# A graph-attention kernel's tile loop: groups of 12 tiles instead of 8, a ring of two groups, one-hots turned by a five-row product

## The chip, the cores and the metric

One core of one Trainium2 chip. The metric is device time in microseconds (us), the median of three runs. The engines go by their names in the profile: PE is TensorE (matrix products; PEld its weight loads), DVE is VectorE, ACT is ScalarE, POOL is GpSimd, SP is SyncE. A name with a q (ACTq) is that engine's instruction queue.

## The reference

A graph-attention layer with four heads over 12,500 nodes and 200,000 edges, added to its input and layer-normalised:

```
feats  = relu(x @ W1 + b1) @ W2 + b2
hid    = relu(concat(feats[row], feats[col], weight) @ A1 + ab1)
e      = leaky_relu(hid @ A2 + ab2, 0.2);   w = exp(e - max(e))
pooled = segment_sum(w * feats[col], row) / (segment_sum(w, row) + 1e-10)
out    = layernorm(x + concat_heads(pooled))
```

## The kernel before, in words

Ahead of the loop the kernel computes two tables over the nodes, one for the row side (`p_table`) and one for the column side (`qf_table`, 776 numbers a node: 516 of the hidden layer, 260 of the features), and sorts the edges by windows of 125 row nodes. A tile is 128 edges of one window, one edge on each partition. There are 1,664 tiles.

The tile loop takes groups of 8 tiles (`SB`), with a ring of 24 tile slots, so of three groups. A step `k` of the loop has one piece on each engine, and the pieces work on different groups, because each engine's instructions stand in one fixed order and meet others only by semaphores. In step `k`:

- POOL gathers the table rows of group `k+1` tile by tile from `qf_table` (L761); each waits until the sum of the tile that held its slot is done.
- ACT makes the one-hots of group `k+1`: edge by window node, four tiles at a time (`onehots`: four Abs L1220, a small copy L1222, one Relu L1224). PE turns them by four transposes (`turn`, L1016), and ACT takes the turned ones out of PSUM (`take_turned`, L1209). The three last rows of a turned one-hot (125 to 127) hold the edge weight in three parts and come with the transposes.
- PE forms the hidden layer of group `k` tile by tile (`hidden_src`: six products of the turned one-hot with the window's table L1003, two with the gathered rows L1007). At the first tile of each four it waits for `take_turned`. DVE adds the gathered half to it (L1596) and takes four dot products (L1606).
- For group `k-1` DVE finds the new running maximum, the shift: three small operations beside tile 0, two beside tile 1 (L1632, L1636), two beside tile 2 (`new_shift` L1642, `shifted` L1646). PE helps twice, after its tiles 2 and 3 (`max_t` L1022, `max_to_all` L1027). Then ACT takes exponentials (`exps`, L1198) and weights the features tile by tile, four activations a tile (`weight`, L1191).
- PE sums the weighted features of group `k-2` by the one-hot (`sum_up`, L990), tile `j` beside its hidden tile `j`, and DVE adds the sums into the window's accumulator (L1655).

ACT's order within a step is: `take_turned(0,1)`, `onehots(1,0)`, `exps`, the load of the records two groups ahead (L1229), then the eight `weight`s, with `take_turned(1,0)` behind the first and `onehots(1,1)` behind the fifth. In a call such as `take_turned(0,1)` the first number is the group relative to `k`, the second the batch of four tiles in it. SP loads the next window's table (L596) as windows are finished. After the loop the shifts of all groups correct the accumulators, and the layer norm follows.

Of the kernel before, what the change touches and what calls it, by code (L numbers as in the profile page):

```python
# [25 lines left out]
I32 = mybir.dt.int32  # L26
# [4 lines left out]
def gnn_layer(nc, x, src, dst, weight, W1, b1, W2, b2, A1, ab1, A2, ab2, out):  # L31
# [30 lines left out]
    SB = 8  # L62
    RING = 24
    SPB = RING // SB
    NT = (E + W * (P - 1)) // P
    NT = -(-NT // SB) * SB
    NSB = NT // SB
    BODIES = NSB // SPB - 1
# [3 lines left out]
    HALF_SB = SB // 2  # L72
# [14 lines left out]
    CHUNKS = NT * P // S  # L87
    sorted_rows = nc.dram_tensor("sorted_rows", (CHUNKS + 3 * P, SF), F32, kind="Internal").ap()
    records = nc.dram_tensor("records", (P * NT, 4), F32, kind="Internal").ap()
    base_rows_d = nc.dram_tensor("base_rows", (BLOCKS, 2, CB * W), BF16, kind="Internal").ap()  # L90
    shift_rows = nc.dram_tensor("shift_rows", (NSB, H), F32, kind="Internal").ap()

    ctx = ExitStack()
    with ctx:
# [14 lines left out]
        iota_row = sb("iota_row", [P, WN])  # L109
# [4 lines left out]
        onehot = sb("onehot", [P, RING, P])  # L114
        onehot_t = sb("onehot_t", [P, SB, P], BF16)
        rec = sb("rec", [P, RING, 4])
# [10 lines left out]
        shift_all = sb("shift_all", [P, NSB, H])  # L127
        last_sb = sb("last_sb", [P, W], I32)
        end_prev = sb("end_prev", [1, W], I32)
        win_pack = sb("win_pack", [1, NT // 4], I32)  # L130
# [3 lines left out]
        win_of = onehot[0:1, :, :].rearrange("p t n -> p (t n)").bitcast(I32)[:, 0:NT]  # L134
        row_tmp = onehot_t[0:1, :, :].rearrange("p t n -> p (t n)").bitcast(I32)[:, 0:NT // 4]
        assert NT <= RING * P
# [105 lines left out]
        rec_all = z[:, 0:NT * 4].rearrange("p (t n) -> p t n", n=4)  # L242
# [5 lines left out]
        shift_flat = shift_all[:, :, :].rearrange("p s h -> p (s h)")  # L248
# [18 lines left out]
        s_row_field = sem("s_row_field")  # L267
# [20 lines left out]
        s_win_iota = sem("s_win_iota")  # L288
        s_stage = [sem(f"s_stage{n}") for n in range(4)]
        s_field_mm = sem("s_field_mm")  # L290
        s_dst_low = sem("s_dst_low")
        s_field_a = sem("s_field_a")
        s_field_b = sem("s_field_b")
        s_rec_st = sem("s_rec_st")
# [5 lines left out]
        s_passed_c = sem("s_passed_c")  # L300
# [10 lines left out]
        s_bias_part = sem("s_bias_part")  # L311
# [13 lines left out]
        s_rec = [sem(f"s_rec{n}") for n in range(SPB)]  # L325
        s_row_dist = sem("s_row_dist")
        s_onehot = sem("s_onehot")
# [28 lines left out]
        s_c_const = sem("s_c_const")  # L356
# [17 lines left out]
        SC = next(NSB // n for n in range(1, NSB) if NSB % n == 0 and NSB // n <= P)  # L374
        KS = NSB // SC
# [38 lines left out]
        N_TAB_STEPS = 13  # L414
# [5 lines left out]
        BULK = NT // P  # L420
        assert BULK * P == NT
# [64 lines left out]
        def _(sp):  # L486
# [86 lines left out]
            for g in range(BULK):  # L573
                sp.wait_ge(s_field_a, g + 1)
                sp.wait_ge(s_field_b, g + 1)
                sp.dma_start(rec_d[:, g * P * 4:(g + 1) * P * 4], rec_all[:, g * P:(g + 1) * P, :].rearrange("p t n -> p (t n)")).then_inc(s_rec_st, 16)
                if g + 4 < BULK:
                    sp.wait_ge(s_field_mm, g + 1)
                    load_stage(g + 4)
            sp.wait_ge(s_a_rows, 16 * 6)  # L580
            sp.wait_ge(s_tab_step, N_TAB_STEPS)
            sp.wait_ge(s_rec_st, 16 * BULK)
            sp.dma_start(rec[:, 0:SB, :].rearrange("p t n -> p (t n)"), rec_d[:, 0:SB * 4]).then_inc(s_rec[0], 16)
            sp.wait_ge(s_rec[0], 16)
# [18 lines left out]
            sp.wait_ge(s_shift_all, NSB)  # L603
            sp.dma_start(shift_rows.rearrange("(a s) h -> a (s h)", a=1), shift_flat[0:1, :]).then_inc(s_c_shifts, 16)
# [16 lines left out]
        def _(pool):  # L621
# [7 lines left out]
            pool.iota(iota_row[:, :], [[1, WN]], base=1, channel_multiplier=0, allow_small_or_imprecise_dtypes=True).then_inc(s_const, 1)  # L629
# [13 lines left out]
            pool.tensor_scalar(minus_b, ident[:, :], -1.0, None, ALU.mult).then_inc(s_bias_part, 1)  # L643
# [3 lines left out]
            pool.wait_ge(s_masks, 1)  # L647
# [4 lines left out]
            pool.tensor_scalar(fields[0:EP, :, 0], edge_t[0:EP, :], 1.0, None, ALU.add).then_inc(s_row_field, 1)  # L652

            pool.wait_ge(s_weights, N_W)
            pool.wait_ge(s_row_field, 1)
# [11 lines left out]
            pool.wait_ge(s_masks, 2)  # L667
# [27 lines left out]
            pool.tensor_copy(hml[rows3, 0, :], bias).then_inc(s_bias_part, 1)  # L695
            pool.wait_ge(s_bias_part, 2)
            pool.tensor_tensor(rest[rows3, 0, :], bias, hml[rows3, 0, :], ALU.subtract).then_inc(s_bias_part, 1)
            pool.wait_ge(s_bias_part, 3)
            pool.tensor_copy(hml[rows3, 1, :], rest[rows3, 0, :]).then_inc(s_bias_part, 1)
            pool.wait_ge(s_bias_part, 4)  # L700
            pool.tensor_tensor(hml[rows3, 2, :], rest[rows3, 0, :], hml[rows3, 1, :], ALU.subtract).then_inc(s_bias_part, 1)
            pool.wait_ge(s_bias_part, 5)
            pool.tensor_scalar(rest[rows3, 0, :], hml[rows3, 0, :], ident[rows3, 0:1], None, ALU.mult).then_inc(s_bias_part, 1)
            pool.wait_ge(s_bias_part, 6)
            pool.tensor_scalar(rest[rows3, 1, :], hml[rows3, 1, :], ident[rows3, 1:2], None, ALU.mult).then_inc(s_bias_part, 1)
            pool.wait_ge(s_bias_part, 7)
            pool.tensor_tensor(rest[rows3, 0, :], rest[rows3, 0, :], rest[rows3, 1, :], ALU.add).then_inc(s_bias_part, 1)
            pool.wait_ge(s_bias_part, 8)
            pool.tensor_scalar(rest[rows3, 1, :], hml[rows3, 2, :], ident[rows3, 2:3], None, ALU.mult).then_inc(s_bias_part, 1)
            pool.wait_ge(s_bias_part, 9)  # L710
# [1059 lines left out]
```

## Time and profile before

| | |
|---|---|
| median of 3 runs | 4588.38 us (4586.27 to 4588.84) |
| the profiled execution | 4587.18 us, span of its instructions 4585.4 us |
| mean granted TensorE clock | 0.977 of full speed |
| the tile loop | from about 1312 us to 4468 us of the span |

The span is the time from the first to the last instruction; the execution's own time is 1.8 us longer. An engine's busy time says how much work it has; which engine sets the time of a stretch is read from who waits for whom there.

### The profile page before, as it was taken

To read this page: it belongs to the slowest core of one execution; us is meant where nothing else is said; L and a number is where in the kernel's file an instruction comes from. 1 tells how busy PE (TensorE), PEld (TensorE's weight loads), DVE (VectorE), ACT (ScalarE), POOL (GpSimd) and SP (SyncE) were. 2 spreads that over 40 slices of the span, in tenths; PEclk is the share of its full clock that TensorE was granted. 3 is DMA by queue.
4 is the path that set the end of the run, shared out by engine and by line. 5 is a ranking of instruction groups with operands and counts; after the bars stand their busy time and mean duration, and the time that the engine had idled before them with its cause. 6 is when DMAs were issued, how large, how long until landed. Compare 5 with 4: busy or idle time off the path is not lost.

```text
span 4585.4 us, 128801 instructions
## 1 busy us (share of the span) xinstructions
PE 4132.6 (90%) x25516; PEld 2946.2 (64%) x25517; DVE 4094.2 (89%) x21278; ACT 3319.3 (72%) x11283; POOL 2340.7 (51%) x2495
## 2 busy tenths in 40 slices
PE   2599999999889999999999999999999999999990
PEld 1255555555567777777777777777777777777760
DVE  8888888888779999999999999999999999999988
ACT  1244444444468888888888888888888888888875
POOL 5444444444445555555555555555555555555535
PEclk9799999999989999999999999999999999999995
DMA  2144444444477777777777777777777777777757
GB/s 90 42 99 89 104 96 91 102 96 93 99 220 224 228 223 226 222 224 226 225 224 223 225 227 221 225 225 226 226 220 223 227 226 223 223 226 224 218 157 224
DMA packets 266911, 851.78 MB, mean 186 GB/s; under 512 B 107916, under 2 KB 109584, under 8 KB 266861
## 3 DMA queue, kind: packets, MB, share of 16 engines
q0 software_dynamic: 169920, 673.54, 52.8%
q1 hardware_dynamic: 63543, 160.18, 11.7%
q10 hardware_dynamic: 33398, 17.49, 1.5%
q8 instruction: 20, 0.33, 0.0%
q14 instruction: 30, 0.25, 0.0%
HBM read 739.10 MB, written 111.90 MB: 186 GB/s over the span
## 4 chain that ended last, share of the span: by engine, by line
PE 38%; ACT 28%; issue 3%; DVE 2%; DMA 0%; ACTq 0%; POOL 0%; DVEq 0%; SPq 0%; POOLq 0%
ACT z L1191 19%; PE psum L1003 16%; PE psum L1007 9%; PE psum L990 9%; ACT onehot L1220 4%; ACT onehot_t L1209 3%; PE psum L1016 3%; ACT onehot L1224 2%; PE psum L971 1%; DVE z L1727 1%; DVE z L1720 1%; PE psum L1027 0%; ACT onehot L1222 0%; DVE z L1743 0%; DVE z L1738 0%
## 5 line engine op out<-in xcount | busy, mean ns | idle before, releaser
L761 POOL DMA_INDIRECT z<-qf_table,rec x1664 | 1605.9, 965 | 1458.8 <-PE psum L990 1038.6
L1191 ACT ACTIVATE z<-z 128x64 f32<-128x64 f32 x6656 | 1651.1, 335 | 0.0
L1003 PE MATMUL psum<-p_win,onehot_t 128*128 x9984 | 1409.7, 274 | 87.2 <-ACT onehot_t L1209 67.0
L1003 PEld LDWEIGHTS psum<-p_win,onehot_t 128*128 128x128 bf16 x9984 | 966.5, 97 | 541.6 <-issue 213.0
L990 PE MATMUL psum<-z,onehot 128*128 128x260 f32 x3328 | 1031.9, 392 | 3.8 <-DVE acc L1655 3.5
L1007 PE MATMUL psum<-z,ident 128*128 128x258 f32 x3328 | 1002.2, 383 | 0.0
L1606 DVE SCALAR_TENSOR_TENSOR z<-z,a_b 128x129 f32<-128x129 f32 x3328 | 881.4, 289 | 3.7 <-issue 0.2
L1606 DVE SCALAR_TENSOR_TENSOR z<-psum,a_b 128x129 f32<-128x129 f32 x3328 | 827.5, 286 | 0.0
L721 POOL DMA_INDIRECT sorted_rows<-z x300 | 475.0, 1583 | 635.9 <-DVE z L1484 487.3
L1596 DVE TENSOR_TENSOR z<-z,psum 128x258 f32<-128x258 f32 x1664 | 698.0, 419 | 98.5 <-PE psum L1007 97.2
L1655 DVE TENSOR_TENSOR acc<-acc,psum 125x260 f32 x1664 | 701.5, 422 | 26.2 <-PE psum L990 4.1
L990 PEld LDWEIGHTS psum<-z,onehot 128*128 128x128 f32 x3328 | 577.2, 190 | 97.5 <-DVE acc L1655 24.7
L1209 ACT ACTIVATE onehot_t<-psum 128x512 bf16<-128x512 f32 x416 | 243.6, 586 | 444.3 <-PE psum L1016 444.3
L1220 ACT ACTIVATE onehot<-iota_row,rec 128x125 f32<-128x125 f32 x1664 | 525.6, 389 | 19.3 <-PE psum L990 13.4
L1007 PEld LDWEIGHTS psum<-z,ident 128*128 128x128 f32 x3328 | 501.9, 190 | 20.4
L1426 DVE TENSOR_REDUCE z<-psum 125x4 f32<-125x400 f32 x400 | 229.0, 572 | 186.8 <-PE psum L833 182.9
L868 PE MATMUL psum<-acc 128*128 128x500 f32 x800 | 377.4, 593 | 0.0
L1111 ACT ACTIVATE acc<-psum,acc 128x500 f32<-128x500 f32 x200 | 135.6, 678 | 279.5 <-PE psum L868 279.5
L1471 DVE TENSOR_TENSOR acc<-z 125x1280 bf16<-125x1280 bf16 x400 | 327.0, 818 | 1.9 <-issue 1.9
L1133 ACT ACTIVATE acc<-psum 125x516 bf16<-125x516 f32 x300 | 181.6, 605 | 184.1 <-PE psum L896 104.7
L1016 PE MATMUL psum<-ident,onehot 128*128 128x128 f32 x1664 | 261.5, 280 | 55.9 <-ACT onehot L1224 55.9
L1224 ACT ACTIVATE onehot<-onehot,ones_f 128x500 f32<-128x500 f32 x416 | 298.1, 717 | 0.0
(230 smaller groups left out, 4602.9 us busy)
## 6 DMA issues: line engine op xcount, KB each, us to landing
p_table<-acc SPq DMA_DIRECT2D x100, 338.6 KB
p_win<-p_table SPq DMA_DIRECT2D x100, 338.6 KB
z<-qf_table,rec POOLq DMA_INDIRECT x1664, 4.5
qf_table<-acc SPq DMA_DIRECT2D x75, 339.5 KB
acc<-in_x_dram SPq DMA_DIRECT2D x25, 448.0 KB
z<-in_x_dram SPq DMA_DIRECT2D x20, 560.0 KB
out_dram<-z ACTq DMA_DIRECT2D x20, 560.0 KB
qf_table<-z SPq DMA_DIRECT2D x25, 339.5 KB
```

What stands on the lines that cost most here:

```text
L721: pool.indirect_dma_start(out=sorted_rows, out_offset=bass.IndirectOffsetOnAxis(ap=row_i[0:KB[k], (b - 3) % 2, k:k + 1], axis=0), in_=rows ...
L761: pool.indirect_dma_start(out=z_t[:, o + j, :], out_offset=None, in_=qf_table, in_offset=bass.IndirectOffsetOnAxis(ap=rec[:, o + j, 3:4].b ...
L990: pe.matmul(psum[:, 4 + j % 2, 0:H * HF], onehot[:, slot, :], z_t[:, slot, ZW:QW], start=True, stop=True)\
L1003: mm = pe.matmul(to, onehot_t[:, j, :], p_flat[:, bass.ds((w % 2) * (3 * ZW) + (part * ZW + o), n)], start=(part == 0), stop=(part == 2 an ...
L1007: mm = pe.matmul(z_two(slot), ident[:, :], z_t[:, slot, NA:ZW], start=False, stop=True, skip_group_check=True)
L1016: mm = pe.transpose(psum[:, 6, j * P:(j + 1) * P], onehot[:, ((k + off) * SB + u * HALF_SB + j) % RING, :], ident[:, :])
L1191: op = act.activation(z_t[:, slot, o:o + DO], z_t[:, slot, o:o + DO], ACT.Copy, scale=z_t[:, slot, o + DO:o + HF])
L1220: op = act.activation(onehot[:, oo + j, 0:WN], iota_row[:, :], ACT.Abs, scale=-1.0, bias=rec[:, oo + j, 0:1])
L1224: act.activation(onehot[:, oo:oo + HALF_SB, 0:WN], onehot[:, oo:oo + HALF_SB, 0:WN], ACT.Relu, scale=-1.0, bias=ones_f[:, 0:1]).then_inc(s ...
L1596: dve.tensor_tensor(own, own, z_one(slot), ALU.add).then_inc(s_z_added, 1)
L1606: return dve.scalar_tensor_tensor(out=own, in0=of, scalar=0.0, in1=a2_b[:, h * AT:(h + 1) * AT], op0=ALU.max, op1=ALU.mult, accum_out=e_ra ...
L1655: dve.tensor_tensor(a, a, psum[0:WN, 4 + j % 2, 0:H * HF], ALU.add).then_inc(s_acc, 1)
```

## The change

Groups have 12 tiles (three batches of four), and the ring of 24 slots holds two groups. The tiles become 1,668 and the groups 139. The transposes go: PE makes the turned one-hot by one product of five rows, since 1 - (e - n)^2 = 2ne - e^2 + 1 - n^2 is 1 where edge row e is node n and at most 0 elsewhere. The five rows of the edges (e, and e^2 in two parts, with two rows of ones) are loaded for a whole group by `load_edges`; ACT's `take_turned` becomes a Relu out of PSUM. The three rows of edge weights no longer come with it: each `take_turned` sends a DMA of three rows by four tiles into rows 125 to 127 (`s_edge_w`), and PE waits for it at the first tile of the batch. The one-hot that is not turned is made a group later, just before it is used (`onehots` works on group `k-1`, the small copy is gone), from rows that `load_rows` loads. The chain to the new shift is spread over DVE's tiles 0, 2 and 3 and PE's tiles 3 and 4. PE's and DVE's sums run seven tiles behind the group's start: tile `j` of group `k-1` beside tile `j+7` of step `k`, the last seven in the next step. Records shrink from four numbers to two, and are loaded one group ahead. The stage that writes records ahead of the loop writes the new rows too.

```diff
-    SB = 8
+    SB = 12
+    BATCH = 4
+    NBATCH = SB // BATCH
+    LAG = 7
     RING = 24
...
                 def gather(j):
...
-                    if live(i, k, -2):
-                        pool.wait_ge(s_agg, tile(-2, j) + 1)
+                    if live(i, k, -1):
+                        pool.wait_ge(s_agg, tile(-1, j) + 1)
...
                 def hidden_src(j):
...
-                    if j % HALF_SB == 0:
-                        pe.wait_ge(s_oht, (i * SPB + k) * 2 + (j // HALF_SB + 1))
+                    if j % BATCH == 0:
+                        pe.wait_ge(s_oht, (i * SPB + k) * NBATCH + (j // BATCH + 1))
+                        pe.wait_ge(s_edge_w[j // BATCH], (i * SPB + k) * 16 + 16)
...
                 def turn(off, u):
-                    for j in range(HALF_SB):
-                        mm = pe.transpose(psum[:, 6, j * P:(j + 1) * P], onehot[:, ((k + off) * SB + u * HALF_SB + j) % RING, :], ident[:, :])
-                    mm.then_inc(s_oht_mm, 1)
+                    if u == 0:
+                        pe.wait_ge(s_edge_k[kn], i * 16 + ((k + off) // SPB + 1) * 16)
+                    since(pe, s_oht, batch)
+                    pe.matmul(psum[0:WN, 6, 0:BATCH * P], node_k[:, 0:WN], edge_k[:, kn, u * BATCH:(u + 1) * BATCH, :].rearrange("p t n -> p (t n)"),
+                              start=True, stop=True).then_inc(s_oht_mm, 1)
...
-                if live(i, k, -3):
-                    sum_up(-3, SB - 1)
                 for j in range(SB):
                     if live(i, k, 0):
                         hidden_src(j)
-                    if j == SB // 4 and live(i, k, 0):
+                    if j == 2 and live(i, k, 0):
                         turn(0, 1)
-                    if j == SB // 4 and live(i, k, -1):
+                    if j == 3 and live(i, k, -1):
                         max_t()
-                    if j == SB // 4 + 1 and live(i, k, -1):
+                    if j == 4 and live(i, k, -1):
                         max_to_all()
-                    if j == SB - SB // 4 and live(i, k, 1):
+                    if j == 6 and live(i, k, 0):
+                        turn(0, 2)
+                    if j == 10 and live(i, k, 1):
                         turn(1, 0)
...
-                    if j < SB - 1 and live(i, k, -2):
-                        sum_up(-2, j)
+                    if j < LAG and live(i, k, -2):
+                        sum_up(-2, j + SB - LAG)
+                    if j >= LAG and live(i, k, -1):
+                        sum_up(-1, j - LAG)
...
                 def take_turned(off, u):
...
+                    act.dma_start(onehot_t[WN:P, own, :],
+                                  row_feats[bass.ds(tile(off, u * BATCH), BATCH), 3:6, :].rearrange("t f n -> f t n")).then_inc(s_edge_w[u], 16)
+                    act.wait_ge(s_oht_mm, batch + 1)
+                    act.activation(onehot_t[0:WN, own, :].rearrange("p t n -> p (t n)"), psum[0:WN, 6, 0:BATCH * P], ACT.Relu).then_inc(s_oht, 1)
...
+                def load_edges():
+                    act.dma_start(edge_k[0:3, kn, :, :], row_feats[bass.ds((i * SPB + (k + 1)) * SB, SB), 0:3, :].rearrange("t f n -> f t n"))\
+                       .then_inc(s_edge_k[kn], 16)
...
+                if live(i, k, -1):
+                    onehots(0)
+                if live(i, k, 1):
+                    load_edges()
                 if live(i, k, 0):
                     take_turned(0, 1)
-                if live(i, k, 1):
-                    onehots(1, 0)
                 if live(i, k, -1):
                     exps()
-                if live(i, k, 2):
+                if live(i, k, 1):
                     load_records()
                 for j in range(SB):
                     if live(i, k, -1):
                         weight(j)
-                    if j == 0 and live(i, k, 1):
+                    if j in (3, 7) and live(i, k, -1):
+                        onehots(j // BATCH + 1)
+                    if j == 3 and live(i, k, 0):
+                        take_turned(0, 2)
+                    if j == 7 and live(i, k, 1):
+                        load_rows()
                         take_turned(1, 0)
-                    if j == SB // 2 and live(i, k, 1):
-                        onehots(1, 1)
...
-                chain = {0: [(-1, bias), (-1, leaky), (-1, tiles_max)], 1: [(-1, heads_max), (-1, diagonal)],
-                         2: [(-1, new_shift), (-1, shifted)]}
+                chain = {0: [(-1, bias), (-1, leaky), (-1, tiles_max)], 2: [(-1, heads_max), (-1, diagonal)],
+                         3: [(-1, new_shift), (-1, shifted)]}
```

## Rows read from the trace of the kernel before

**Rows 1.** The page's first part: busy us, share, instructions of each engine.
```profile
PE 4132.6 (90%) x25516; PEld 2946.2 (64%) x25517; DVE 4094.2 (89%) x21278; ACT 3319.3 (72%) x11283; POOL 2340.7 (51%) x2495
```

**Rows 2.** 2000:3000: busy PE, PEld, DVE, ACT, POOL, clock, DMA share, GB/s; L1655's group.
```profile
2000.00:3000.00 1000.00, 957.52 (x6034) 725.54 (x6033) 934.26 (x5899) 854.86 (x3176) 544.40 (x663) 1.00 0.77 224
...
L1655 DVE TENSOR_TENSOR acc<-acc,psum 125x260 f32 x531 | 223.9, 422 | 6.8
```

**Rows 3.** Timeline, ScalarE, one group of 8: start, us, engine, line, what [idle before].
```profile
2501.68 0.60 ACT L1209 ACTIVATE onehot_t<-psum 128x512 bf16<-128x512 f32 x1 [1.91 <-PE psum L1016]
...
2502.17 3.92 ACT L1191 ACTIVATE z<-z 128x64 f32<-128x64 f32 x16
...
2505.99 1.26 ACT L1220 ACTIVATE onehot<-iota_row,rec 128x125 f32<-128x125 f32 x4
...
2510.77 0.57 ACT L1209 ACTIVATE onehot_t<-psum 128x512 bf16<-128x512 f32 x1
...
2511.34 1.27 ACT L1220 ACTIVATE onehot<-iota_row,rec 128x125 f32<-128x125 f32 x4
...
2512.64 0.72 ACT L1224 ACTIVATE onehot<-onehot,ones_f 128x500 f32<-128x500 f32 x1
...
2512.78 0.34 ACTq L1229 DMA_DIRECT2D rec<-records  x1
...
2513.26 0.24 ACT L1198 ACTIVATE z<-e_sh 128x32 f32<-128x32 f32 x1
...
2513.54 1.06 ACT L1191 ACTIVATE z<-z 128x64 f32<-128x64 f32 x4
...
2516.78 0.60 ACT L1209 ACTIVATE onehot_t<-psum 128x512 bf16<-128x512 f32 x1 [2.18 <-PE psum L1016]
```

**Rows 4.** Timeline, TensorE and VectorE, the same group.
```profile
2509.10 0.82 PE L1003 MATMUL psum<-p_win,onehot_t 128*128 x6
...
2511.09 0.19 DVE L1646 TENSOR_TENSOR e_sh<-e_val,shift 128x32 f32<-128x32 f32 x1
...
2511.78 0.94 PE L1003 MATMUL psum<-p_win,onehot_t 128*128 x6 [0.48 <-ACT onehot_t L1209]
...
2512.99 0.60 PE L990 MATMUL psum<-z,onehot 128*128 128x260 f32 x2
...
2513.43 0.82 PE L1003 MATMUL psum<-p_win,onehot_t 128*128 x6
...
2514.97 0.82 PE L1003 MATMUL psum<-p_win,onehot_t 128*128 x6
```

**Rows 5.** DMA view, ScalarE's queue: packets from 2512.78 to 2514.28, 2515.28, 2515.78.
```profile
q10 hardware_dynamic: 1, 0.00, 0.1%
...
q10 hardware_dynamic: 78, 0.01, 2.5%
...
q10 hardware_dynamic: 144, 0.02, 3.8%
```

**Rows 6.** The chain of waits, two transfers outside the tile loop: start, us.
```profile
1310.41 1.78 DMA rec<-records
...
4468.45 1.16 DMA shift_rows<-shift_all
```

**Rows 7.** DMA view, 704.08 to 705.33, ScalarE's queue, one two-row load.
```profile
q10 hardware_dynamic: 4, 0.01, 2.3%
```

**Rows 8.** Line 761, the gathers, 2000 to 3000 us.
```profile
DMA to landing us min/median/max: 3.8/4.5/7.1
```

**Rows 9.** TensorE by timeline, by chain, by windows (busy, granted clock, DMA share, GB/s).
```profile
1303.65 2.84 PE L971 MATMUL psum<-ident,z 128*128 128x128 f32 x12
...
1316.42 1.47 PE psum L1003 x6
...
1307.50:1310.00 2.50, 0.00 (x0) 0.78 0.28 105
...
1317.50:1320.00 2.50, 2.50 (x12) 0.67 0.94 340
```

More of the change, by code:

```diff
@@ L373, in gnn_layer @@
         CR = 5
-        SC = next(NSB // n for n in range(1, NSB) if NSB % n == 0 and NSB // n <= P)
-        KS = NSB // SC
+        SC = next(NSH // n for n in range(1, NSH) if NSH % n == 0 and NSH // n <= P)
+        KS = NSH // SC
         assert CGROUPS * CG == W and CGROUPS % CR == 0
@@ L413, in gnn_layer @@
         N_PARTS = 5
-        N_TAB_STEPS = 13
+        N_TAB_STEPS = 14
+        assert SB == 12 and all(t * 683 >> 13 == t // SB for t in range(NT))
         EMPTY_W = CHUNKS // P * SF
@@ L702, in _ @@
[L702 to L707, printed above, removed]
@@ L1203, in take_turned @@
                 def take_turned(off, u):
-                    group = (i * SPB + (k + off)) * 2 + u
-                    act.wait_ge(s_oht_mm, group + 1)
+                    batch, own = (i * SPB + (k + off)) * NBATCH + u, slice(u * BATCH, (u + 1) * BATCH)
                     if live(i, k, off - 1):
-                        act.wait_ge(s_z_mm, tile(off - 1, u * HALF_SB + HALF_SB - 1) + 2)
-                    act.activation(onehot_t[:, u * HALF_SB:(u + 1) * HALF_SB, :].rearrange("p t n -> p (t n)"),
-                                   psum[:, 6, 0:HALF_SB * P], ACT.Copy).then_inc(s_oht, 1)
@@ L1212, in onehots @@
-                def onehots(off, u):
-                    group = (i * SPB + (k + off)) * 2 + u
-                    oo = ((k + off) * SB + u * HALF_SB) % RING
-                    act.wait_ge(s_rec[(k + off) % SPB], i * 16 + ((k + off) // SPB + 1) * 16)
-                    if live(i, k, off - 3):
-                        act.wait_ge(s_agg, tile(off - 3, u * HALF_SB + HALF_SB - 1) + 1)
-                    for j in range(HALF_SB):
-                        op = act.activation(onehot[:, oo + j, 0:WN], iota_row[:, :], ACT.Abs, scale=-1.0, bias=rec[:, oo + j, 0:1])
+                        act.wait_ge(s_z_mm, tile(off - 1, u * BATCH + BATCH - 1) + 2)
@@ new lines, in take_turned, with onehots @@
+                    act.dma_start(onehot_t[WN:P, own, :],
+                                  row_feats[bass.ds(tile(off, u * BATCH), BATCH), 3:6, :].rearrange("t f n -> f t n")).then_inc(s_edge_w[u], 16)
+                    act.wait_ge(s_oht_mm, batch + 1)
+                    act.activation(onehot_t[0:WN, own, :].rearrange("p t n -> p (t n)"), psum[0:WN, 6, 0:BATCH * P], ACT.Relu).then_inc(s_oht, 1)
+                def onehots(u):
+                    batch, own, kn = (i * SPB + (k - 1)) * NBATCH + u, slice(u * BATCH, (u + 1) * BATCH), (k - 1) % SPB
+                    if u == 0:
+                        act.wait_ge(s_row_e[kn], i * 16 + ((k - 1) // SPB + 1) * 16)
+                    if live(i, k, -2):
+                        act.wait_ge(s_agg, tile(-2, u * BATCH + BATCH - 1) + 1)
+                    for j in range(u * BATCH, (u + 1) * BATCH):
+                        op = act.activation(onehot[:, j, :], iota_row[:, :], ACT.Abs, scale=-1.0, bias=row_e[:, kn * SB + j:kn * SB + j + 1])
```

269 lines of the change are left out of this document (168 added, 101 removed).

## The prediction

> **What bounds the kernel now.** I read the page's first part, then the windows, then the timeline of one group. The first part names no bound: PE, DVE and ACT are all busy most of the time [rows 1]. In a steady stretch of the tile loop 531 tiles take 1000 us, so 1.883 us a tile and 15.07 us a group of 8, with PE busy 0.96, DVE 0.93 and ACT 0.85 of it [rows 2]. Undisturbed, PE needs 1.54 us a tile [rows 4], so 12.3 us of the 15.07. The rest is a ping-pong, which the timeline shows: ACT stands idle 1.9 to 2.2 us before L1209, for PE's transposes, and PE 0.48 us before L1003, for L1209 [rows 3, 4]. From one such L1209 to the next is 15.1 us [rows 3]. So neither engine's sum of work sets the time; the order in which PE and ACT meet does, and the change must be judged by the chain it builds, not by the work it saves.
>
> **What the change takes away.** Four transposes become one product of 512 columns. The small copy goes from ACT, but the Relu behind it starts 1.30 us after the first Abs, when the last Abs is done (1.27 us), so the copy already lay in that wait and its removal gives nothing [rows 3]. The per-group chain on DVE is paid every 12 tiles instead of every 8. All of this is relief for engines that wait.
>
> **The chain that it builds.** Read the new order as a circle. `exps` waits for `shifted` on DVE beside tile 3; that waits for `max_to_all`, which PE issues behind its hidden tile 4. Tile 4 opens batch 1, so PE waits there for `take_turned(0,1)` and for its three weight rows. ACT issues both just ahead of the same `exps`, and only after all the weights and one-hots of the step before. So in each step ACT sends the rows, then waits until they have landed, PE has done tile 4 and DVE the shift. Nothing hides that. Before, `max_to_all` stood behind tile 3, which opens no batch.
>
> I add up one turn, with 0 at the start of `exps`.
>
> First ACT: `exps` to the first weight takes 0.28 us, and the records' DMA is now issued between them by an ACT with nothing queued, so most of its 0.34 us shows: 0.58 [rows 3]. Four tiles of weights take 3.82 (2502.17 to 2505.99), Abs and the wait 1.30 [rows 3]: the Relu of `onehots(1)` starts at 5.70. The next DMA goes out 0.14 us behind the start of a Relu [rows 3]: the rows of batch 2 leave at 5.84 and land D2 later.
>
> Then PE: it restarts 0.45 us after what it waited for (L1209 from 2510.77 lasts 0.57, L1003 starts at 2511.78) [rows 3, 4]. It does tile 8 with its sum (1.21 + 0.44), tile 9 (1.54), tile 10 (1.10) and the turning product, which I estimate at 0.3 from the first of these: 4.59 us [rows 4]. ACT waits for that product in `take_turned(1,0)`.
>
> Then ACT again: 0.05 to be released, `take_turned` 0.49, weights of tiles 8 to 11 3.82, Abs and wait 1.30, and 0.48 until `load_edges` has been issued ahead of the rows of batch 1 (0.14 + 0.34) [rows 3]. They land D1 later, and PE restarts, 0.45.
>
> Last, from L1003 of the tile ahead of `max_to_all` to the end of `shifted` is 2.18 us (2509.10 to 2511.28) [rows 4], 2.2 to the next `exps`.
>
> Sum: 5.84 + D2 + 0.45 + 4.59 + 0.54 + 5.12 + 0.48 + D1 + 0.45 + 2.2 = 19.67 + D1 + D2.
>
> **How long a row transfer takes.** The trace has no such transfer in the loop. Nearest is ACT's own load of records (128 rows of 128 bytes): one packet is done 1.5 us after its issue, 78 of 144 after 2.5, all after 3.0 [rows 5]. Outside the loop the same load took 1.78 us, and a small store 1.16 [rows 6]; in the loop the DMA engines are 77% busy with gathers [rows 2]. The records' 144 packets are nine on each of 16 engines. A load of two rows makes four packets [rows 7], two of data and two completions, so rows decide how many engines work; three rows then go to three engines, four pieces and a completion each. Five packets at that pace (1.5 us for nine, after the first 1.5) end at 2.3, and with 0.2 for the release D2 = 2.5. Batch 1's rows stand behind `load_edges` in the same queue, three rows of twelve pieces, so there are 18 packets on each of those engines: 1.5 + 3.0 + 0.2 - 0.34 for the earlier start = 4.4. Where the gathers pause they go faster; I take D1 = 3.9, between that and the 3.0 of the records. Bounds: 1.16 for both below; 3.5 and 6 above, were each packet as slow as the records' slowest.
>
> The Trainium skill, DMA: Bandwidth & Descriptors, section "Why a DMA increments its semaphore by 16 and not by 1", says that the number of engines is the largest, up to 16, that divides the slowest dimension of both sides, which for three rows is three; the two-row load agrees. The same page, section "Anatomy of one DMA — SWDGE (gpsimd) path", gives about 2.0 us fixed for a small transfer; the 1.78 agrees, the loop's 3.0 does not, and by 2.0 for both the time would be the 4771 of the first rival.
>
> So a turn is 19.67 + 2.5 + 3.9 = 26.07 us for 12 tiles, 2.17 us a tile. 139 turns are 3624 us against 208 x 15.07 = 3135: +489. Behind the last hidden tile ACT has four more weighted tiles (3.8) and three one-hot batches of 1.92 (5.8) to do: +10. The stages ahead of the loop change by a few small operations and transfers in both directions; I take 0 and allow 5 us. The sum is 4587.2 + 499 = 5086 us, made against the profiled execution's own 4587.18, which is 1.2 under the median; I predict 5085.
>
> **Costed at nothing.** Gathers: a slot is freed by the sum at position j+7 and needed at position j+12, four tiles and a part later, 6.8 us at PE's own 1.54 and over 8 at 2.17; a gather lands in 4.5, at most 7.1 us [rows 8]. With that cover gone (a loop near 1.6 us a tile) the slow ones would show. POOL issues one a tile as before. Batch 0's rows leave 6.2 us after batch 2's and land, behind `load_rows`, about when PE comes to tile 0. The new records' load holds POOL's first gather, which the sum at position 7 holds as long. DVE has 21.1 us of work at its present 1.76 a tile [rows 2], under the turn.
>
> **Rivals.** *Short transfers*: rows land in 2.0 us and three engines are no hindrance. Then ACT's own DMA issues and PE's walk through tiles 8 to 4 set the turn, 23.8 us: +173 + 10, 4771 us. For it: rows 6; against: rows 5. Even at 1.16 the turn is 23.0 and the time 4658.
>
> *A slower clock*: PE would stand idle some 3.7 us before each tile 8. After the last product ahead of the loop (1306.49) the granted clock was 0.78 in the window to 1310, so it fell to the lower level, 1.2 GHz, about 2.4 us later; work began again at 1316.42, and 0.67 in the window from 1317.5 puts the return near 1319.1 [rows 9]. Half speed over 2.7 us loses 1.35 us before the product that ACT waits for: turn 27.4, 5274 us. Against: most idle stretches in the new loop are shorter. The Trainium skill, TensorE: Matmul & The Clock Gate, section "What's actually happening", says the same of the two levels, that idleness brings the lower; by that rule this rival holds.
>
> *Faster*: the rows land under ACT's Relu and `take_turned`, within about 0.9 us of issue, and the DMA issues lie under queued work. The turn is then ACT's 19.4 us of work, its release of PE (0.45) and 2.2 back, 21.9 us: 4506. It decides below a turn of 22.49 us, (3135 - 10)/139. No transfer in the trace lands so soon.
>
> *No change to be measured*: the same with issues exposed, 22.4 us, 4575 to 4580.
>
> **Numbers.** Forecast as summed, 46%, by itself 4900 to 5230; short transfers 18%; slower clock 25%; faster 7%; no change 4%. The range leaves out the two last and the far end of slow transfers: 4740 to 5340. A difference under 0.2% can't be told from none. Faster 0.08, same 0.03, slower 0.89.
>
> **What would show it.** ACT idle before the exponentials for some 5 us in every group, released by DVE's `shifted`; PE idle before the products of tiles 4 and 8, released by a DMA into `onehot_t` and not by ACT; a group near 26 us; ACT's share of the loop near 0.75, PE's lower than before. It is wrong if PE is found waiting at tile 4 for nothing, if the row transfers land in under 1.2 us, or if a group takes less than 22.5 us.

## The result, and the profile after

The changed kernel takes 5351.76 us (median of 4 runs, 5349.72 to 5364.36), the kernel before, beside it, 4588.1: a ratio of 1.167 (95% interval 1.165 to 1.169). Slower was forecast, and 5085 us, with a range up to 5340; the measured time lies 12 us above it.

The page's first part, and the windows view of the same stretch as in [rows 2] (busy PE, PEld, DVE, ACT, POOL; clock, DMA share, GB/s):

```profile
PE 4382.2 (82%) x24024; PEld 2907.4 (54%) x24025; DVE 4023.7 (75%) x20702; ACT 3311.9 (62%) x10764; POOL 2306.3 (43%) x2410
...
2000.00:3000.00 1000.00, 833.53 (x4452) 575.32 (x4451) 729.38 (x4555) 677.78 (x2396) 418.84 (x494) 0.92 0.63 179
```

Every engine has a smaller share than in [rows 1, 2]: no engine became the bound, all wait more. The line of the exponentials says where; first before, then after (duration, first and last start, shape):

```profile
L1198 ACT ACTIVATE z<-e_sh x208: 238/245/262, 1335.7 to 4456.1; 128x32 f32<-128x32 f32 x104
```

```profile
L1255 ACT ACTIVATE z<-e_sh x139: 291/292/295, 1342.8 to 5215.6; 128x48 f32<-128x48 f32 x139
```

From first to last the loop takes 3872.8 us instead of 3120.4, 752.4 of the 765.1 by which the span grew (5350.5 against 4585.4). The first exponentials come 7.1 us later and 5.6 us more follow the last. The loop itself begins 4.5 us earlier (PE's first hidden product at 1311.9 and not at 1316.4); four more tiles stand ahead of the first exponentials. A turn, from one group's exponentials to the next, is 3872.8 / 138 = 28.06 us for 12 tiles; before it was 3120.4 / 207 = 15.07 for 8, or 22.6 for 12.

The timeline of ACT over one turn of 27.54 us, to be held against [rows 3]:

```profile
2499.75 0.29 ACT L1255 ACTIVATE z<-e_sh 128x48 f32<-128x48 f32 x1 [4.77 <-DVE e_sh L1722]
...
2505.51 0.72 ACT L1281 ACTIVATE onehot<-onehot,ones_f 128x512 f32<-128x512 f32 x1
2505.74 0.25 ACTq L1265 DMA_DIRECT2D onehot_t<-row_feats  x1
...
2515.37 0.60 ACT L1268 ACTIVATE onehot_t<-psum 125x512 bf16<-125x512 f32 x1 [2.92 <-PE psum L1070]
2515.86 3.92 ACT L1248 ACTIVATE z<-z 128x64 f32<-128x64 f32 x16
...
2520.98 0.72 ACT L1281 ACTIVATE onehot<-onehot,ones_f 128x512 f32<-128x512 f32 x1
2521.20 0.25 ACTq L1294 DMA_DIRECT2D rows_k<-row_feats  x1
2521.70 0.25 ACTq L1265 DMA_DIRECT2D onehot_t<-row_feats  x1
2522.07 0.60 ACT L1268 ACTIVATE onehot_t<-psum 125x512 bf16<-125x512 f32 x1 [0.37 <-PE psum L1070]
2527.29 0.29 ACT L1255 ACTIVATE z<-e_sh 128x48 f32<-128x48 f32 x1 [4.63 <-DVE e_sh L1722]
```

and of PE in the same turn, where [rows 4] had 0.48 us of idle time before L1003, for ACT:

```profile
2508.85 1.15 PE L1057 MATMUL psum<-p_win,onehot_t 128*128 x6 [3.69 <-DMA onehot_t<-row_feats]
...
2523.76 0.68 PE L1043 MATMUL psum<-z,onehot 128*128 128x260 f32 x2
2525.03 0.95 PE L1057 MATMUL psum<-p_win,onehot_t 128*128 x6 [0.59 <-DMA onehot_t<-row_feats]
```

The chain of waits in that turn has the two transfers with their durations:

```profile
2505.74 2.59 DMA onehot_t<-row_feats
...
2521.70 2.79 DMA onehot_t<-row_feats
```

The reader is to see four things. The rows of batch 2 leave only after four weights and a batch of one-hots (2505.74), and PE stands 3.69 us for them before tile 8. Then ACT stands 2.92 us for PE (2515.37). Then the rows of batch 1 leave behind the rest of ACT's work (2521.70), and PE has waited 0.59 us for them at tile 4. Then ACT has waited 4.63 us for the shift. That is the circle of the forecast. And the clock, in windows across the first stall (columns as above):

```profile
2507.00:2509.00 2.00, 0.15 (x2) 0.12 (x2) 0.00 (x0) 2.00 (x9) 0.21 (x1) 1.00 0.81 228
2509.00:2510.00 1.00, 1.00 (x7) 0.84 (x7) 0.00 (x0) 1.00 (x6) 0.00 (x0) 0.73 0.41 168
2510.00:2511.00 1.00, 1.00 (x4) 0.81 (x3) 0.10 (x1) 1.00 (x5) 0.00 (x0) 0.50 0.00 0
...
2513.00:2514.00 1.00, 1.00 (x8) 0.77 (x7) 0.52 (x2) 0.00 (x0) 0.69 (x2) 1.00 0.04 5
```

PE was idle from 2505.2; the granted clock was still full to 2509, fell to 1.2 GHz about 0.6 us after work had begun again (by the 0.73 of the second line), and was back at 2.4 GHz at 2513. So the first products after the stall ran at half speed, though the stall itself was at full. That order is this turn's and not the rule: of the 35 stalls before tile 8 between 2000 and 3000 us the clock fell in 34, from 2.1 to 4.8 us after PE's last product, and in 21 of them before work began again. So it was ahead of the tile 8 that starts at 2480.15:

```profile
2478.00:2479.00 1.00, 0.00 (x0) 0.00 (x0) 0.00 (x0) 1.00 (x5) 0.00 (x0) 0.87 0.95 276
2479.00:2480.00 1.00, 0.00 (x0) 0.00 (x0) 0.00 (x0) 1.00 (x5) 0.00 (x0) 0.50 0.64 261
```

In either order PE paid for it: in those 34 cases 3.7 us on average of the work behind the stall ran at 1.2 GHz.

The DMA view (queue, kind: packets, MB, share of 16 engines) shows what the rows meet: first batch 2's rows, from issue to landing (2505.74 to 2508.33), beside the gathers (q0); then batch 0's, the same size, sent at 2512.49 behind the 144 packets of `load_rows` and landed at 2513.95, with no gather moving:

```profile
q0 software_dynamic: 98, 0.48, 77.9%
q10 hardware_dynamic: 15, 0.00, 0.6%
...
q10 hardware_dynamic: 159, 0.01, 7.2%
```

The first took 2.59 us and the second 1.46. From 2000 to 3000 us the medians, by the updates of the transfers' semaphores, are 1.42 us for batch 0, with the DMA engines 13% busy on average in the 1.4 us behind its issue, 2.67 for batch 2 at 65%, and 3.00 for batch 1 at 73%.

### The profile page after: what moved, and what is told of

It reads as the page before. It is cut to its first block, busy times and chain, and to the rows that moved or that the text cites. A ratio compares the mean times of both kernels' runs of the same rounds, so it can differ in the third digit from the quotient of the medians.

```text
span 5350.5 us, 127363 instructions
## 1 busy us (share of the span) xinstructions
PE 4382.2 (82%) x24024; PEld 2907.4 (54%) x24025; DVE 4023.7 (75%) x20702; ACT 3311.9 (62%) x10764; POOL 2306.3 (43%) x2410
## 4 chain that ended last, share of the span: by engine, by line
PE 35%; ACT 20%; DMA 11%; issue 5%; DVE 3%; ACTq 2%; POOL 0%; DVEq 0%; SPq 0%; POOLq 0%
PE psum L1057 15%; ACT z L1248 14%; DMA onehot_t<-row_feats 11%; PE psum L1061 9%; PE psum L1043 8%; ACT onehot L1278 4%; PE psum L1070 1%; PE psum L1081 1%; ACTq L1285 1%; ACT onehot_t L1268 1%; DVE z L1807 1%; DVE z L1682 1%; DVE z L1800 0%; DMA p_win<-p_table 0%; DVE shift L1718 0%
## 5 line engine op out<-in xcount | busy, mean ns | idle before, releaser
L1057 PE MATMUL psum<-p_win,onehot_t 128*128 x10008 | 1541.0, 291 | 618.7 <-DMA onehot_t<-row_feats 567.6
L1057 PEld LDWEIGHTS psum<-p_win,onehot_t 128*128 128x128 bf16 x10008 | 1015.1, 101 | 1190.7 <-issue 850.1
L1043 PE MATMUL psum<-z,onehot 128*128 128x260 f32 x3336 | 1142.6, 426 | 23.2 <-issue 16.8
L1061 PE MATMUL psum<-z,ident 128*128 128x258 f32 x3336 | 1083.2, 408 | 3.6 <-DMA z<-qf_table,rec 3.6
L1043 PEld LDWEIGHTS psum<-z,onehot 128*128 128x128 f32 x3336 | 618.5, 203 | 251.1 <-issue 162.9
L1061 PEld LDWEIGHTS psum<-z,ident 128*128 128x128 f32 x3336 | 547.4, 205 | 33.1 <-DMA z<-qf_table,rec 4.5
L1268 ACT ACTIVATE onehot_t<-psum 125x512 bf16<-125x512 f32 x417 | 246.3, 591 | 505.7 <-PE psum L1070 505.3
L1278 ACT ACTIVATE onehot<-iota_row,row_e 128x128 f32<-128x128 f32 x1668 | 527.2, 388 | 0.0
L1255 ACT ACTIVATE z<-e_sh 128x48 f32<-128x48 f32 x139 | 40.6, 292 | 689.8 <-DVE e_sh L1722 689.8
L1281 ACT ACTIVATE onehot<-onehot,ones_f 128x512 f32<-128x512 f32 x417 | 301.0, 722 | 13.6
```

The costliest lines, as they stand in the source:

```text
L1043: pe.matmul(psum[:, 4 + j % 2, 0:H * HF], onehot[:, j, :], z_t[:, slot, ZW:QW], start=True, stop=True)\
L1057: mm = pe.matmul(to, onehot_t[:, j, :], p_flat[:, bass.ds((w % 2) * (3 * ZW) + (part * ZW + o), n)], start=(part == 0), stop=(part == 2 an ...
L1061: mm = pe.matmul(z_two(slot), ident[:, :], z_t[:, slot, NA:ZW], start=False, stop=True, skip_group_check=True)
L1278: op = act.activation(onehot[:, j, :], iota_row[:, :], ACT.Abs, scale=-1.0, bias=row_e[:, kn * SB + j:kn * SB + j + 1])
```

## The experiments

Twelve kernels were run. The turn is worked out for each as above, from the first and the last exponentials of its trace; the ratio is to the kernel before, run beside it, whose median was 4588.1 to 4588.5 us.

| kernel | us | ratio (95%) | turn us |
|---|---|---|---|
| changed kernel | 5351.76 | 1.167 (1.165–1.169) | 28.06 |
| e1_max_early | 5221.36 | 1.138 (1.136–1.140) | 27.13 |
| e2_rows_early | 4827.64 | 1.053 (1.052–1.055) | 24.26 |
| e3_both | 4714.77 | 1.028 (1.026–1.029) | 23.50 |
| e4_fill | 5172.85 | 1.128 (1.126–1.130) | 26.73 |
| e5_edges_late | 5378.87 | 1.172 (1.170–1.174) | 28.24 |
| e6_all_three | 4618.17 | 1.007 (1.005–1.008) | 22.72 |
| e7_turned_early | 5202.38 | 1.134 (1.132–1.136) | 26.97 |
| e8_rows_turned | 4750.91 | 1.036 (1.034–1.038) | 23.67 |
| e9_four | 4519.18 | 0.985 (0.983–0.987) | 22.04 |
| e10_swap | 5260.23 | 1.146 (1.144–1.148) | 27.41 |
| e11_four_late_max | 4533.82 | 0.988 (0.987–0.990) | 22.16 |
| e12_before_late_max (groups of 8) | 4735.27 | 1.032 (1.031–1.034) | 15.77 |

**The two places of the circle, one at a time and together.** e1 puts the maximum ahead of the tile that opens batch 1:

```diff
                 for j in range(SB):
+                    if j == 4 and live(i, k, -1):
+                        max_to_all()
                     if live(i, k, 0):
                         hidden_src(j)
...
-                    if j == 4 and live(i, k, -1):
-                        max_to_all()
```

> One part changed from the kernel after: PE issues max_to_all ahead of hidden tile 4 instead of behind it, so the exponentials no longer wait for the rows of batch 1. The kernel after takes 28.3 us a group, 139 groups, and 1415 us outside. Circle theory: the turn loses the landing of batch 1's rows; what is left runs from exps over the rows of batch 2, PE's tiles 8 to 3 and the shift back to exps: 23.5 us if the clock holds, 25.2 if it falls as before, so 4680 to 4920 us. Rival, that the DMAs' latency counts once per batch wherever the chain stands, or that the clock is the cause: within 1% of 5352. Rival, more tiles per group cost it by themselves: 5352.

e2 takes the rows' DMA out of `take_turned` into `send_rows` and issues each one `take_turned` earlier:

```diff
+                    send_rows(0, 2)
                     take_turned(0, 1)
...
+                    if j == 3 and live(i, k, 1):
+                        send_rows(1, 0)
                     if j == 3 and live(i, k, 0):
                         take_turned(0, 2)
                     if j == 7 and live(i, k, 1):
                         load_rows()
+                        send_rows(1, 1)
                         take_turned(1, 0)
```

> One part changed from the kernel after: each DMA of three weight rows is issued one take_turned earlier, so about four tiles ahead of its use; the order of everything else stays. Circle theory: both landings (2.6 and 2.8 us) leave the turn and with them PE's long idle stretches and the lower clock; exps still waits for PE's tile 4 and that for take_turned, so the turn is ACT's 19.9 us of work, 0.5 until PE restarts and 2.3 back: 22.7 us, 4570 us, at most 4700 if some rows still land late. Rival, the transfers are hidden and something else (gathers with a shorter lead, more groups' worth of work) sets the time: over 5200.

e3 is both:

> Both edits of the two kernels before it together: rows sent one batch earlier, max_to_all ahead of hidden tile 4. Circle theory: no engine waits for a round trip any more, the turn is the largest sum of work, DVE's 20.6 to 21.2 us, so 4280 to 4360 us, faster than the kernel before the change (4588). Rival, a second chain of the same length stands behind the first (gathers with a lead of five tiles, the two-group ring): 4570 or more, like the kernel with the rows alone.

All three went in the direction expected, and all three fell short of it: -0.93, -3.80 and -4.56 us a turn. The time of e3 is the one of its rival, a second chain (4570 or more), but the gathers named there as its cause are not: PE waits 5.4 us for them in the whole run. With one circle only the three should have gained more, so my theory lacked something. The trace of e3 shows it (ACT and PE, one turn):

```profile
2520.43 0.29 ACT L1255 ACTIVATE z<-e_sh 128x48 f32<-128x48 f32 x1 [3.99 <-DVE e_sh L1732]
...
2526.84 0.58 ACT L1274 ACTIVATE onehot_t<-psum 125x512 bf16<-125x512 f32 x1
...
2544.07 0.29 ACT L1255 ACTIVATE z<-e_sh 128x48 f32<-128x48 f32 x1 [3.14 <-DVE e_sh L1732]
```

```profile
2523.61 0.42 PE L1070 MATMUL psum<-rows_k 5*125 5x512 bf16 x1
...
2527.85 0.95 PE L1057 MATMUL psum<-p_win,onehot_t 128*128 x6 [1.65 <-ACT onehot_t L1274]
...
2541.28 0.27 PE L1076 MATMUL psum<-ident,tile_max 128*4 128x128 f32 x1
```

A second circle needs no transfer: from the exponentials through four weights and a batch of one-hots to the Relu of batch 2 and PE's start of tile 8 (2527.85, 7.42 us), then PE's tiles 8 to 11 and 0 to 3 and the way back over the shift (16.22 us): 23.64 us, that whole turn. The product that the Relu reads had ended at 2524.03; ACT came to it 2.81 us later because of the order written out for it. In the changed kernel this circle is nearly as long as the forecast one: PE waits only 0.59 us at tile 4 (0.66 on average over the run), so whatever shortens the forecast circle behind tile 8 gains no more than some 0.6 us before the second one holds. e1 (-0.93) is of that size; e2 shortens both. e1 also took tile 4 out of the way to the shift, 1.3 us, and got little for it: DVE's order took its place. The waits of DVE for the maximum over the whole run, in the changed kernel and in e1 (us, times, longest):

```profile
DVE shift L1718 <- PE psum L1081: 164.3, 136, 4.6
...
DVE shift L1718 <- PE psum L1081: 0.3, 1, 0.3
```

In e1 DVE comes to the shift only behind its own dot products of tile 3, when the maximum is already there.

**The clock alone.** e4 gives PE 20 products of 380 columns into a free PSUM region ahead of tile 8, so that it is busy while the rows land; nothing else is changed.

```diff
                 for j in range(SB):
+                    if j == 8 and live(i, k, 0):
+                        for _ in range(20):
+                            pe.matmul(psum[:, 7, P + H:512], ones_b[:, :], iota_win[:, :, :].rearrange("p a n -> p (a n)")[:, 0:512 - P - H],
+                                      start=True, stop=True)
```

> The kernel after with 20 products of 380 columns added on PE ahead of hidden tile 8, into a part of PSUM that nothing reads; they take about 3.2 us, in which PE stands idle in the kernel after. Clock theory: the granted clock stays at full speed over tiles 8 to 10, which then take 4.6 us instead of 6.5, and the turn falls by 1.9 to 26.4 us: 5090 us, the forecast's sum without the slower clock. Rival, the clock is not on the path: within 0.5% of 5352. If the products last longer than the idle stretch, somewhat above 5352.

The windows view of e4:

```profile
2000.00:3000.00 1000.00, 942.21 (x5456) 640.73 (x5454) 769.80 (x4825) 719.36 (x2542) 445.25 (x524) 1.00 0.67 190
```

The clock is 1.00 in this stretch, and useless work makes the kernel 179 us faster: 1.33 us a turn is the clock's price in the changed kernel, net of what the products cost. The kernel is 83 us slower than the 5090 expected: with the products in it the stall is longer, 3.38 us of them and 0.56 of idle time on average against 3.66.

**What stands ahead in the queue.** e5 moves `load_edges` from ahead of batch 1's rows to behind the records' load.

> The changed kernel with load_edges moved from ahead of the rows of batch 1 to behind the records' load, so that nothing stands ahead of those rows in ACT's queue. If the queue's order cost what the prediction charged (D1 3.9 against D2 2.5, and 0.34 of issue): 1.4 to 1.7 us a turn, 5115 to 5160 us. If standing behind the 36 pieces costs next to nothing, as the 2.8 us against 2.6 in the trace of the changed kernel say: the issue and 0.2 us, 0.3 to 0.5 us a turn, 5280 to 5310 us.

It got slower by 27 us, and neither case held. A turn of e5 on ACT:

```profile
2506.82 0.29 ACT L1255 ACTIVATE z<-e_sh 128x48 f32<-128x48 f32 x1 [4.54 <-DVE e_sh L1721]
...
2513.24 0.25 ACTq L1265 DMA_DIRECT2D onehot_t<-row_feats  x1
...
2530.54 0.25 ACTq L1265 DMA_DIRECT2D onehot_t<-row_feats  x1
...
2536.22 0.29 ACT L1255 ACTIVATE z<-e_sh 128x48 f32<-128x48 f32 x1 [4.29 <-DVE e_sh L1721]
```

From the issue of batch 1's rows to the exponentials it took 5.68 us in a turn of e5 (2530.54 to 2536.22) and 5.59 in the changed kernel (2521.70 to 2527.29): standing behind `load_edges` had cost the rows nothing that shows. Over the whole run they land in 3.27 us on average in e5 and in 3.11 in the changed kernel. The issue did cost; but moved behind the exponentials it stands on the same circle, where ACT has nothing queued either: batch 2's rows now leave 6.42 us after the exponentials (2506.82 to 2513.24) and not 5.99.

**The second circle.** e7 leaves the maximum as it is and moves the two `take_turned`, with the rows' transfers in them, forward on ACT, each ahead of a batch of one-hots; e6 does it on top of e3, e8 on top of e2.

```diff
-                    if j == 3 and live(i, k, 0):
+                    if j == 2 and live(i, k, 0):
                         take_turned(0, 2)
                     if j == 7 and live(i, k, 1):
                         load_rows()
+                    if j == 6 and live(i, k, 1):
                         take_turned(1, 0)
```

> The changed kernel with the two moves on ACT alone (the take_turned of batch 2, with its rows' transfer, behind the third weight, that of the next group's batch 0 behind the seventh). Theory of the first circle: rows of batch 2 leave 3.6 us after the exponentials and not 5.9, tile 8 starts 2.3 us earlier, but ACT has the same work to do until it sends the rows of batch 1, so the turn loses only what ACT stood waiting for the turning product, 0.9 us, and whatever of the slow clock at tile 8 goes with the shorter stall was in that wait already: turn 27.4 us, 5150 to 5290 us, about 5225. Rival, that the second circle alone sets the turn: 2.3 us less in each, about 5030 us; that the clock's loss at tile 8 comes on top, 4900.

> As the run with all three edits, but the maximum stays behind hidden tile 4, as in the changed kernel. Theory: with the rows' transfers and the second circle gone, what is left of the first circle is ACT's own order: from the exponentials all 12 weights, three batches of one-hots and three Relus (20.4 us), PE's restart at tile 4 (0.45) and the way back to the exponentials (2.26), a turn of 23.1 us; 4560 to 4700 us, about 4625. Rival, that the place of the maximum costs nothing once the rows are early: the same time as the run with all three edits.

> Both earlier edits together (the all-heads maximum ahead of tile 4, the weight rows sent one batch earlier), and on ACT the Relu of batch 2 now stands behind the third weight and that of the next group's batch 0 behind the seventh, each ahead of a batch of one-hots. Theory of a second circle (the exponentials, ACT's weights and one-hots, the Relu of batch 2 or of batch 0, PE's eight tiles from there to the maximum, the exponentials again; 7.4 + 16.2 us in the trace of both edits, 23.7 measured): PE finds batch 2 ready when tile 7 is done, and the turn falls from 23.7 us to what ACT (20.4) and PE (20.9) have to do in it, 21 to 21.6; time 4340 to 4430 us, about 4400, and faster than the kernel before. Rival, that the gathers or DVE hold the loop at 23.7 us: no change against both edits, 4680 to 4730 us.

e7 met its number, 1.09 us a turn less and not 2.3; PE's stall for rows has gone from tile 8 to tile 4 (3.34 us on average). e8 and e6 came in above theirs. The second circle is gone from e6 (PE waits for no Relu at tile 8), but PE still waits at tile 4 for the Relu of batch 1, as in this turn:

```profile
2519.64 0.60 ACT L1274 ACTIVATE onehot_t<-psum 125x512 bf16<-125x512 f32 x1 [0.31 <-issue]
...
2520.67 0.96 PE L1057 MATMUL psum<-p_win,onehot_t 128*128 x6 [1.17 <-ACT onehot_t L1274]
```

From 2000 to 3000 us PE's idle time there is 0.84 us on average. In 38 of the 44 turns PE starts tile 4 just 0.43 us after that Relu has ended, though the profile names the Relu in only 14 of them and mostly DVE in the others. ACT waits up to 1.1 us for the other two turning products, 53.3 us in those 44 turns (15.9 in e9). The rival, no gain over e3, fell too (-0.78 us a turn).

**One exchange on ACT.** In the changed kernel a batch of one-hots stands ahead of `take_turned(0,1)`, and nothing between it and `exps`. e10 exchanges the two; e9 does it on top of e6, and puts the other two Relus directly ahead of their batches of one-hots.

```diff
+                if live(i, k, 0):
+                    take_turned(0, 1)
                 if live(i, k, -1):
                     onehots(0)
                 if live(i, k, 1):
                     load_edges()
-                if live(i, k, 0):
-                    take_turned(0, 1)
                 if live(i, k, -1):
                     exps()
```

> The changed kernel with one exchange on ACT: take_turned of batch 1, with its rows, ahead of the one-hots of batch 0 and not behind them. The rows of batch 1 then leave 1.9 us earlier and land while PE is at tiles 2 and 3, but their Relu still waits for the turning product behind tile 2, and PE's tiles 3 and 4 and the way back stay on the circle: from the trace about 26.4 us where that circle took 27.5, so the mean turn goes from 28.3 to about 27.2 us, 5130 to 5240 us, about 5195. If instead the whole of the landing were the cost (2.8 + 0.5 us): 25 us a turn, 4890 us. If something else held tile 4: no change, 5340 to 5365 us.

> The run with all three edits, and on ACT every Relu of a batch now stands directly ahead of a batch of one-hots: that of batch 1 ahead of the one-hots of batch 0 and not behind them, those of batch 2 and of the next batch 0 behind the fourth and the eighth weight. In the trace of all three edits PE still waits 1.17 us at tile 4 for the Relu of batch 1, and ACT 0.5 to 1.1 us each for the turning products of the other two. Theory, that these two waits are what is left of the meetings of ACT and PE: both go, the turn falls from 22.8 us to 21.6 to 22.2 (PE alone has 20.9), 4430 to 4560 us, about 4500, faster than the kernel before. Rival, that PE's other small waits (gathers, DVE's release of PSUM) take their place: 4590 to 4640 us, as before.

e10 gained 0.65 us a turn, 20 us short of its range: PE's wait at tile 4 is gone, and that wait was 0.66 us on average. e9 met its range and beats both kernels: 1.5% below the kernel before. Its windows view and two meetings on ACT:

```profile
2000.00:3000.00 1000.00, 973.29 (x5706) 695.16 (x5707) 924.78 (x5845) 870.24 (x3075) 539.21 (x634) 1.00 0.79 230
```

```profile
2512.87 0.29 ACT L1255 ACTIVATE z<-e_sh 128x48 f32<-128x48 f32 x1 [1.75 <-DVE e_sh L1733]
...
2517.33 0.57 ACT L1274 ACTIVATE onehot_t<-psum 125x512 bf16<-125x512 f32 x1
```

PE is busy 0.97 of the stretch, and the Relu of batch 2 waits for nothing. ACT still stands 1.75 us for the shift, but PE has no wait for ACT left in this stretch: its idle time at tile 4 is 0.18 us and not 0.84, which is 0.66 of the 0.68 us by which the turn fell from e6.

**A tile more in the chain to the shift.** e12 does that part of the change alone, in the kernel before; e11 undoes e1's edit in e9.

```diff
-                    if j == SB // 4 + 1 and live(i, k, -1):
+                    if j == SB // 4 + 2 and live(i, k, -1):
                         max_to_all()
...
-                         2: [(-1, new_shift), (-1, shifted)]}
+                         3: [(-1, new_shift), (-1, shifted)]}
```

> The kernel before, groups of 8, with one part of the change alone: the new shift found over one tile more (max_to_all behind PE's hidden tile 4, which opens a batch here too; new_shift and shifted beside DVE's tile 3). In its trace the shift is done at 2511.28 us and the exponentials start at 2513.26, because a batch of one-hots stands between the Relu of batch 1 and them on ACT; the shift would come some 2.7 us later, and ACT waits 2.18 us a little later in the group anyway. Theory, that the late shift costs only where nothing stands between the Relu of batch 1 and the exponentials: 0 to 0.3 us a group of 8, 4585 to 4650 us, about 4590. Rival, that a tile more in the chain is paid in full wherever it stands (0.7 us of it shows behind the 2.0 of slack, or the whole 2.7): 4730 to 5150 us.

> The run with all four edits, with the maximum put back behind hidden tile 4 as in the changed kernel; between the Relu of batch 1 and the exponentials stands now a batch of one-hots. In the trace of all four the exponentials wait 1.75 us for the shift all the same, and the next meeting of ACT and PE is the Relu of batch 2, for which PE has half a tile to a tile of slack. If the later chain is covered as in the groups of 8: 4515 to 4545 us. If a tile more shows past that slack: 0.5 to 1.0 us a turn, 4590 to 4660 us, about 4620, as in the pair without and with the early maximum before (0.95).

e11 held: 15 us, 0.12 a turn. e12 did not: 147 us, 0.70 us a group, the low end of its rival. The waits of e12 (engine, line, what for: us in 1000, times, longest):

```profile
DVE shift L1642 <- PE psum L1027: 59.8, 64, 1.1
PE psum L1003 <- ACT onehot_t L1209: 37.6, 42, 1.0
ACT z L1198 <- DVE e_sh L1646: 32.8, 43, 0.8
```

DVE now stands 0.93 us a group ahead of `new_shift`, and the exponentials wait up to 0.8. Which of the two carries the 0.70 was not tried. What the pair shows is that the place of the maximum has no price of its own: 0.70 us in a group of 8, 0.95 a turn between e8 and e6, 0.12 between e11 and e9.

## Why the prediction was partly right, and what failed

The terms of the turn, as forecast and as the turn at 2499.75 shows them:

| term | forecast | measured |
|---|---|---|
| exponentials to the rows of batch 2 | 5.84 | 5.99 |
| D2 | 2.5 | 2.59 |
| PE's restart | 0.45 | 0.52 |
| tiles 8 to 10 and the turning product | 4.59 | 6.47 |
| release and `take_turned` | 0.54 | 0.54 |
| weights, Abs and wait | 5.12 | 5.12 |
| until batch 1's rows leave | 0.48 | 0.72 |
| D1 | 3.9 | 2.79 |
| PE's restart | 0.45 | 0.54 |
| back to the exponentials | 2.2 | 2.26 |
| sum | 26.07 | 27.54 |

- **The circle** was right: the same links in the same order, found by reading the new order of instructions with the durations of the old trace. PE had to wait for batch 1's rows at tile 4, so that this circle held, in 27 of the 35 turns from 2000 to 3000 us. ACT idle before the exponentials 4.6 to 4.8 us (forecast some 5), PE idle before tiles 4 and 8 for a DMA, ACT's share of the loop 0.68 (forecast 0.75).
- **The step that failed is the one that chose "forecast as summed" over "a slower clock".** The sum itself held a stall of 3.7 us before each tile 8, longer than the 2.4 us after which the clock had fallen in [rows 9]; the argument against, that most idle stretches are shorter, says nothing about the one that is not. The half-speed products stood at nothing in the sum; in the turn above they took 1.88 us. The rival had the mechanism, but its price of 1.35 us was too small: it has 2.7 us at the low clock, the trace 3.7 on average. That e4 gave back 1.33 us, net of what its products cost, and so agrees with the rival, is luck. The Trainium skill, TensorE: Matmul & The Clock Gate, section "What's actually happening", says that idleness brings the lower level; the trace agrees, 0.50 from 2510 to 2512 after 3.69 us of idle time.
- **D1 was mis-sized**, 3.9 for 2.79. The reckoning that the rows wait for 12 pieces each of `load_edges` on the same engines fell: e5 took them away and nothing came faster, and batch 0's rows landed in 1.46 us behind 144 packets. What sets the time is the traffic of the gathers, as far as the runs show: in e2, where batch 0's rows leave earlier and meet the gathers (65% busy and not 13%), they land in 2.60 us and not in 1.42. D2, at the pace beside gathers and without a queue, was right within 0.1. The Trainium skill, DMA: Bandwidth & Descriptors, section "Anatomy of one DMA — SWDGE (gpsimd) path", has about 2.0 us for a small transfer that GpSimd issues; the prediction took it for ACT's. ACT's two here took longer, 2.59 and 2.79, and batch 0's less, 1.46.
- With the clock at its rival's price and D1 as measured the forecast would have been 26.3 us; small starts and restarts add 0.7, the clock in this turn 0.5, and the mean turn is 0.5 above this one, for the most part because rows land later (2.66 and 3.11 us on average over the run; PE's waits for them reach 5.7 us). What makes the latest so late was not tried. So 139 turns of 28.06 and not 26.07 us are 277 us more than the sum.
- **Costed at nothing** held: gathers land in 3.6 to 7.0 us and PE waits 3.6 us for them in the whole run. Ahead of the loop I took 0 and allowed 5, behind it 10. Both together came to nothing: 139 turns of 28.06 less 208 of 15.07 us are already 765.4 of the 765.1 us. With that 10 too much, the 277 above leave the 267 by which 5352 passes 5085.
- **Rivals.** Short transfers fell: 2.6 to 2.8 us, not 2.0, for the two on the circle. The faster case needed rows that land under ACT's work; e2 shows that it was a question of when they are sent (its terms, 19.4, 0.45 and 2.2, add up to 22.05 and not to 21.9 us, so 4527 and not 4506). That earlier rows alone are not enough is shown step by step, in the order in which the edits were added: rows early -3.80 us a turn, maximum early -0.76, Relus early -0.78, Relus ahead of one-hots -0.68, together 6.02, from 28.06 to 22.04.
- **What it half saw** is the second circle. It stands in the prediction only as PE's walk through tiles 8 to 4, which sets the turn in its first rival (23.8 us), and was not set beside the forecast circle. It does not change the forecast of this kernel by more than 0.6 us a turn, but it made my expectations of e1 to e3 too bold; those of e6 and e8 left out the wait at tile 4 that e9 and e10 then took away.

So with the order of e9 the rest of the change leaves 0.57 us per 12 tiles to the good (22.61 to 22.04); the order in which ACT met PE and the transfers cost 6.02. What the larger groups, the five-row product and the smaller records are worth one by one was not tried.

## What to carry to other kernels

When a change reorders engines that run fixed instruction streams, write down every circle through the new order, not only the longest: the gain of an edit that leaves the second one as it is ends where that one begins, and the idle time in front of the meeting point (0.66 us here on average, where e10 gained 0.65) says how far that is. Send a transfer one piece of work before its consumer, and put on the engine that releases another the release first and the unshared work after it. If your own sum contains a stall as long as one after which the trace shows TensorE's clock fallen, the half-speed products behind it are a term of the sum and no rival.

## What was not expected of the hardware

- The clock can fall after a stall has ended: in the turn shown it was full through 3.7 us of idle time and at 0.50 for the products behind it. In 34 of 35 such stalls it fell, and 3.7 us of the work behind them ran at the low clock on average, so a stall costs more than it lasts.
- Twenty useless products a group made the kernel 179 us (3.3%) faster.
- A three-row load of 3 KB, issued by ACT beside gathers, took 2.6 to 2.8 us from issue, and the 36 pieces ahead of it in the same queue made no difference that shows; the same load in a pause of the gathers took 1.46 us behind 144 packets.
